# Gathers of four groups begun in one row, and a hold on the fifth gather and on the second tile's b1 loads

## The reference

```python
x = x + L0(x, language_ids, W, Wr, A, B)     # base product + gated low-rank experts
x = x + L1(x, A, B, adapter_ids)             # one low-rank adapter per batch

# L0
base   = einsum('btd,od->bto', x, W)
logits = einsum('btd,ed->bte', x, Wr) + 5.0 * one_hot(language_ids, 8)
gates  = softmax over the top 2 of 8 logits, 0 elsewhere
h      = einsum('btd,erd->bter', x, A)        # 8 experts of rank 16
L0     = base + 2.0 * einsum('bter,bte,eor->bto', h, gates, B)

# L1
Bx  = einsum('bni,bri->bnr', x, B[adapter_ids])   # 64 adapters of rank 16, "down"
L1  = einsum('bnr,bor->bno', Bx, A[adapter_ids])  # "up"
```

## Time and profile before

| | us |
|---|---|
| median of 3 runs (lowest, highest) | 99.37 (99.19, 99.54) |
| profiled execution | 99.88 |
| its span, first to last instruction | 98.1 |
| PE busy in the span | 92.2 (94%) |
| DVE, ACT, POOL busy | 60.5, 43.7, 36.6 |

### The profile page before, as it was taken

One profiled execution on the slowest core, in us unless ns is written; L12 is line 12 of the kernel. 1 busy time (PEld: TensorE's weight loads), 2 busy tenths in 40 slices (PEclk: granted clock), 3 DMA queues, 4 the chain that ended last, 5 costly groups with the idle time before them and its releaser, 6 DMA issues.

```text
span 98.1 us, 2162 instructions
## 1 busy us (share of the span) xinstructions
PE 92.2 (94%) x733; PEld 77.8 (79%) x733; DVE 60.5 (62%) x215; ACT 43.7 (45%) x88; POOL 36.6 (37%) x44
## 2 busy tenths in 40 slices
PE   4999999999969999999999999999999999999950
PEld 1499888889758888889978897889888898898840
DVE  4146999320767739891089649880199479873970
ACT  2554355939806791089207880199019700001100
POOL 5000780899850049995000079980000460000000
PEclk9999999999999999999999999999999999999999
DMA  1998987339777892237422902247000004150074
GB/s 27 358 302 249 332 301 228 95 83 306 201 225 202 234 298 57 51 68 164 141 64 72 380 4 107 107 55 272 0 0 3 0 0 168 53 213 1 7 258 170
DMA packets 14844, 14.36 MB, mean 146 GB/s; under 512 B 9969, under 2 KB 11249, under 8 KB 14449
## 3 DMA queue, kind: packets, MB, share of 16 engines
q1 hardware_dynamic: 13904, 11.85, 38.5%
q0 software_dynamic: 640, 2.10, 7.7%
q10 hardware_dynamic: 288, 0.28, 0.9%
HBM read 10.02 MB, written 4.19 MB: 145 GB/s over the span
## 4 chain that ended last, share of the span: by engine, by line
PE 88%; DMA 3%; DVE 3%; issue 1%; DVEq 0%
PE main L650 15%; PE main L656 15%; PE main L662 14%; PE aw_ps L692 14%; PE side L744 7%; PE main L677 4%; PE main L676 4%; PE main L678 4%; DMA aws<-aw_t 3%; PE aw_ps L768 3%; PE side L692 3%; DVE xs L540 2%; PE side L724 2%; PE main L768 1%; PE side L768 1%
## 5 line engine op out<-in xcount | busy, mean ns | idle before, releaser
L327 POOL TENSOR_TENSOR x_lo<-xs,x_hi 128x512 fp32r<-128x512 f32 x12 | 15.2, 1300 | 21.3 <-ACT x_hi L348 18.7
L650 PE MATMUL main<-x_hi,w_hi 128*128 128x512 f32 (+1 forms) x64 | 17.7, 397 | 0.0
L656 PE MATMUL main<-x_hi,w_lo 128*128 128x512 f32 (+1 forms) x64 | 16.9, 385 | 0.0
L662 PE MATMUL main<-x_lo,w_hi 128*128 128x512 f32 (+1 forms) x64 | 16.8, 384 | 0.0
L692 PE MATMUL aw_ps<-aws,xs 128*128 128x136 f32 x112 | 14.6, 284 | 0.0
L692 PEld LDWEIGHTS aw_ps<-aws,xs 128*128 128x128 f32 x112 | 14.2, 195 | 0.2
L656 PEld LDWEIGHTS main<-x_hi,w_lo 128*128 128x128 f32 x64 | 11.8, 188 | 2.6
L662 PEld LDWEIGHTS main<-x_lo,w_hi 128*128 128x128 f32 x64 | 11.8, 188 | 2.4
L650 PEld LDWEIGHTS main<-x_hi,w_hi 128*128 128x128 f32 x64 | 11.3, 188 | 2.2
L380 ACT ACTIVATE a_ops<-a_hi 64x512 fp32r<-64x512 f32 x12 | 7.6, 630 | 11.5 <-POOL a_rest L295 11.4
L499 DVE TENSOR_TENSOR xs<-main,xs 128x512 f32<-128x512 f32 x15 | 9.9, 683 | 1.9 <-PE main L678 1.9
(11 more groups left out here) (107 smaller groups left out, 130.8 us busy)
## 6 DMA issues: line engine op xcount, KB each, us to landing
out_t<-xs SPq DMA_DIRECT2D x16, 256.0 KB, 2.3
xs<-x_t SPq DMA_DIRECT2D x3, 1024.0 KB, 5.0
b1s<-b_t SPq DMA_DIRECT2D x64, 32.0 KB, 2.0
xs<-x_t SPq DMA_DIRECT2D x4, 256.0 KB, 4.0
ws<-w_t SPq DMA_DIRECT2D x4, 256.0 KB, 5.0
b0s<-b_t SPq DMA_DIRECT2D x1, 256.0 KB, 4.8
aws<-aw_t ACTq DMA_DIRECT2D x1, 204.0 KB, 4.0
rows<-a_t,row_at POOLq DMA_INDIRECT x8, 4.0
```

The source lines that it names most:

```text
L327: nc.gpsimd.tensor_tensor(x_lo[:, t % 2, c], xs[:, t, c], x_hi[:, t % 2, c].bitcast(F32), ALU.subtract).then_inc(x_lo_ready, 1)
L650: nc.tensor.matmul(out_ap, w_hi[:, c, k], x_hi[:, s, k, n], start=(k == 0), stop=False)
L656: nc.tensor.matmul(out_ap, w_lo[:, c, k], x_hi[:, s, k, n], start=False, stop=False)
L662: last = nc.tensor.matmul(out_ap, w_hi[:, c, k], x_lo[:, s, k, n], start=False, stop=False)
```

## The change

Four gathers instead of two are begun in a row at the start, gather 4 stays where it was but behind a wait, and SP waits ahead of the b1 loads of the second tile. Both waits are for `down_done` to reach 2, which is when the two down products of the first tile are finished.

```diff
@@ SP @@
             for t in range(NB):
+                if t == 1:
+
+                    sp.wait_ge(down_done, GPB)
                 for g in range(t * GPB, (t + 1) * GPB):
                     load_b1(g)
                 if t + 2 < NB:
@@ POOL @@
             pool.wait_ge(row_at_ready, 1)
-            for g in range(GPB):
+            for g in range(SLOTS):
                 gather(g)
@@ POOL, loop over tiles, behind x_lo @@
                 if t == 1:
-                    for g in range(GPB, SLOTS):
-                        gather(g)
+
+                    pool.wait_ge(down_done, GPB)
                 for g in range((t - 1) * GPB, t * GPB):
                     if t > 1:
                         split_a1(g)
```

## The result

| | us | ratio to before (95% interval) |
|---|---|---|
| before, 6 runs beside it (lowest, highest) | 99.37 (99.08, 99.54) | |
| changed kernel, 6 runs (lowest, highest) | 98.16 (97.63, 98.25) | 0.987 (0.984 to 0.990) |
| profiled execution of the changed kernel; its span | 98.09; 96.2 | |

The changed kernel is 1.21 us faster, and the forecast was 98.2. The lines behind SP's new wait are numbered 3 higher than before, so the down products are line 747.

A forecast was written before the change was run, and what follows sets the result against it. TensorE's matmul row bounds the kernel, with one hole in the first down batch. Profiled 99.88 less 1.48 is 98.40; allowing for the 0.51 lower median gave 97.89 to 98.40, taken as 98.2 us; range 97.7 to 99.5.

The forecast's parts named there:

- The 1.48 us taken for the batch: First tile's down products: 2.84 us falls to the second tile's 1.36 us, a gain of 1.48 us.
- the bounds 0.84 and 1.77: First down batch: gain at least the two idle pieces, 0.84 us; at most 1.77 us, limited by VectorE's x1 additions.
- Rival (a): First down batch: only the idle pieces go, short pieces between stay slow; about 98.8 us; chance 0.15.
- Rival (b): First down batch: hole is recording's or PE's supply's, or gathers aren't its cause; 99.37 us, give or take 0.2; chance 0.21.
- The cause named: First down batch: data of gathers 2 to 4 landing slow it; DMA engines 81% busy, gathers' queue 62%; b1 loads less suspect.
- What a gather beside long matmuls costs: Base products beside the moved gathers 2 and 3: long matmuls with operands ready hide the landing data; cost 0.
- POOL's order: POOL: x_lo behind the early gathers starts about 0.1 us late, by 17.9; holding gather 4 costs 0, using idle time.
- SP's order: SP: held b1 loads are last issued near 38.1, first stores start near 59.5; cost 0, with 6.5 us of cover.
- What is late next: After the first down batch: gated tiles end at 30.9, PE's transposes come at 31.36; 0.46 us left, no new wait.
- Rival (c): Before the first down batch: early gathers delay b1 of group 1; slower, 100.2 us at 4.3 us delay; 0.14 with other waits.
- The split of the 0.51 us between profiled execution and median: Whole kernel: recording may slow the first down batch by all 0.51 us (runs lose 0.97) or by none.
- the middle between 97.89 and 98.40: Whole kernel's time: 98.40 if all 0.51 us is recording, 97.89 if none; middle, rounded up a little, 98.2 us.

The follow-up runs named there:

- e7: Changed kernel plus three spare gathers, read by nobody, at the old place of gathers 2 to 4; 99.72 us, ratio 1.003.
- e3: Kernel before with only SP's wait ahead of the second tile's b1 loads, gathers not moved; 99.17 us, ratio 0.997.
- e10: e6 plus one spare gather, read by nobody, issued inside the second down batch; 99.35 us, ratio 0.998.
- e9: Changed kernel plus one spare gather, read by nobody, begun inside the first down batch; 98.49 us, ratio 0.991.
- e1: Kernel before with gathers 0 to 3 begun in one row, no wait added; 97.95 us, ratio 0.986.
- e2: Changed kernel without SP's wait, so b1 of groups 2 and 3 load through the first down batch; 98.11 us, ratio 0.987.
- e4: Kernel before with gathers 2 to 4 held until the first down batch is done, nothing else changed; 98.02 us, ratio 0.985.
- e5: The changed kernel itself, run again as reference in the second set of runs; 98.25 us, ratio 0.989.
- e6: Changed kernel with gathers 5 and 6 moved to be issued just before the second down batch; 98.06 us, ratio 0.988.
- e8: Changed kernel plus three plain 256 KB loads, read by nobody, issued by SP ahead of its wait; 98.14 us, ratio 0.987.
- e12: Changed kernel plus three plain 256 KB loads, read by nobody, issued by POOL at the old place of gathers 2 to 4; 97.53 us, ratio 0.981.
- e11: Changed kernel plus three POOL additions of 128x512, result unread, at the old place of gathers 2 to 4; 102.52 us, no ratio.

## Why the prediction was right, and where it was not

- **The place and the size.** The 1.48 us taken for the batch measured 1.58. It lies between the bounds 0.84 and 1.77. Rival (a), that only the idle pieces go, fails: the short pieces between them became quick too. Rival (b), that the runs don't have the hole or the gathers don't make it, fails: e7 brings it back with gathers alone, and kernels with it in the trace (before, e3, e7, e10) have medians from 99.17 to 99.72, e9 with a smaller one has 98.49, and kernels without (e1, e2, e4, e5, e6, e8, e12, the changed one) from 97.53 to 98.25.
- **The cause named is half right.** The gathers were the suspect and the b1 loads less so: that holds (e3, e7). But the argument went by the landing data, 81% DMA share and 62% for the gathers' queue, and that step fails: e6 has 86%, e8 has 93%, and neither loses anything, while the hole of e9 has 0%. What the runs show in its place is that a hole comes when POOL is issuing a gather during the short matmuls (before, e3, e7, e9, e10), and doesn't when the issue has ended ahead of them (e1, e6) or begins behind them (the change, e4). The sentence that the quick batches have b1 loads but no gather beside them was the better evidence. That the sum held all the same was luck in this respect: a gather that is moved takes its issue and its data with it, so the forecast came out the same by either.
- **What a gather beside long matmuls costs: nothing**, as taken. Four gathers in a row between 12.93 and 17.86 leave PE's base products beside them at 0.91 to 0.92 us for four.
- **POOL's order.** x_lo was to start by 17.9, and started at 17.88. The hold on gather 4 cost nothing, behind an idle time that is still 4.53 us.
- **SP's order.** The last held issue was forecast near 38.1 and ended at 38.20; the first stores came at 58.74 (forecast 59.5). Neither held anything up, and e2 against e5 shows no cost. The rule that the prediction weighed (the Trainium skill, "DMA: Bandwidth & Descriptors", section "Rules for kernel authors": issue early, wait late) found nothing to win either: e2 follows it for the b1 loads and has the time of e5.
- **What is late next.** 0.46 us was forecast between the gated tiles and the transposes; it was 30.99 - 30.68 = 0.31, still no wait.
- **Rival (c)**, the early gathers delaying b1 of group 1, didn't happen: the first batch began at 26.78 without a wait for b1, 0.27 us sooner than before, 0.24 of which the start had brought.
- **From the profile to the median.** The split of the 0.51 us between profiled execution and median was no sound step. The single runs of the kernel before scatter from 99.01 to 99.99 over the three sets, and its profiled execution (99.88) was one of the high ones; nothing shows that recording slows the batch. So the middle between 97.89 and 98.40 had no ground, and that it came within 0.1 us of 98.16 is luck. The gain in medians (1.21) is smaller than that in the two profiled executions (99.88 - 98.09 = 1.79) by that scatter.

**What stays open.** Why the issue of a gather stops PE isn't settled. The profile shows no wait for it, and the stop outlasts the gather's row on POOL by 0.37 us (e9) to 0.8 us (e10). In e9 it is the first long matmul that starts late, so the stop isn't a matter of the short ones alone. Plain loads from the same engine didn't do it, but it began none inside a batch (e12), so whether it takes a gather or any transfer that POOL issues there isn't settled. Why one gather costs 0.46 us (e9) and the third of three costs 1.5 (e7, e10) isn't settled either; in e9 no earlier gather was under way.

## What to carry to other kernels

A hole in a row of short matmuls that the chain calls "issue" is to be compared with the same stretch of another tile, and with what each other engine does at that moment; here a gather that GpSimd was issuing was enough, and it was cured by beginning it a few us earlier or later. When a change removes two suspects at once, put each back alone: the wait on SP, half of this change, was worth nothing. A high DMA share beside a slow stretch is no cause until a run with the same share and other transfers is slow too.

## What the runs showed that was not expected

- An indirect gather of 128 rows issued by GpSimd during 64 short matmuls held TensorE up by 0.46 us (e9) to 1.5 us (e7, e10), in e9 with the DMA engines at rest, while 342 GB/s of plain loads (e8) didn't stop it at all.
- Three additions on GpSimd with two inputs in SBUF held a VectorE subtraction of 128x4 elements, so that it took 3.53 us instead of 0.17 (e11), and GpSimd's x_lo another, so that it took 0.56 (e9). The Trainium skill ("GPSIMD Engine Reference", section "Key points") says that the two engines share SBUF interfaces and collide where VectorE has two SBUF inputs; the rows agree, and the subtraction ended only with the last operation of GpSimd's row.
